# Attention in a gated cross-attention block: image copies on ScalarE, normalising on GpSimd, maxima of two PSUM banks at once

## What is computed

```python
ctx_img, ctx_txt = context[:, :257], context[:, 257:]
q = rms_norm(linear(x, q_w, q_b), norm_q_w)
k, k_img = rms_norm(linear(ctx_txt, ...)), rms_norm(linear(ctx_img, ...))
v, v_img = linear(ctx_txt, v_w, v_b), linear(ctx_img, v_img_w, v_img_b)
def attention(q, k, v):
    scores = jnp.einsum('bqhd,bkhd->bhqk', q, k) / sqrt(32)
    return jnp.einsum('bhqk,bkhd->bqhd', softmax(scores), v)
out = attention(q, k_img, v_img) + attention(q, k, v)
x = x + tanh(g_xattn[0]) * linear(out, o_w, o_b)
```

## Time and profile before

| | |
|---|---|
| Runs (3) | 1731.56 us median (1729.67 to 1732.33) |
| Profiled execution, first to last instruction | 1726.7 us |
| TensorE busy | 1689.0 us, 98%, granted clock at its upper level nearly throughout |
| VectorE | 1201.3 us, 70% |
| GpSimd | 901.7 us, 52% |
| ScalarE | 822.3 us, 48% |

### The profile page before, as it was taken

One profiled execution on the slowest core, in us unless ns is written; L12 is line 12 of the kernel. 1 busy time (PEld: TensorE's weight loads), 2 busy tenths in 40 slices (PEclk: granted clock), 3 DMA queues, 4 the chain that ended last, 5 costly groups with the idle time before them and its releaser, 6 DMA issues. The chain is left out here.

```text
span 1726.7 us, 24755 instructions
## 1 busy us (share of the span) xinstructions
PE 1689.0 (98%) x8694; PEld 1105.9 (64%) x8694; DVE 1201.3 (70%) x2250; ACT 822.3 (48%) x1520; POOL 901.7 (52%) x343
## 2 busy tenths in 40 slices
PE   6999999999999999999999999998999999999999
PEld 5888878885444445444544444445777778888777
DVE  6776677667888887888778888877555354443565
ACT  4433333236666664666556666662322355554221
POOL 3221312116777774787747777711515477675542
PEclk9999999999999999999999999999999999999999
DMA  9556858546555542554545445221313488876533
GB/s 330 165 165 196 229 182 211 180 164 192 138 151 146 145 134 57 147 151 132 148 122 127 111 131 142 84 93 42 134 37 134 159 266 271 261 264 211 166 109 98
DMA packets 198603, 273.04 MB, mean 158 GB/s; under 512 B 30968, under 2 KB 128008, under 8 KB 197964
## 3 DMA queue, kind: packets, MB, share of 16 engines
q1 hardware_dynamic: 192928, 254.61, 50.0%
q0 software_dynamic: 5120, 16.78, 2.9%
q10 hardware_dynamic: 432, 0.07, 0.0%
HBM read 198.15 MB, written 106.18 MB: 176 GB/s over the span
## 5 line engine op out<-in xcount | busy, mean ns | idle before, releaser
L1255 ACT ACTIVATE P<-ps 128x512 f32<-128x512 f32 (+1 forms) x832 | 444.4, 596 | 257.2 <-PE ps L1096 223.0
L640 DVE TENSOR_REDUCE mp<-ps 128x1 f32<-128x448 f32 x768 | 426.9, 613 | 83.9 <-PE ps L443 83.9
L1521 POOL TENSOR_TENSOR sacc<-sacc,P 128x2048 f32<-128x2048 f32 x90 | 396.3, 4403 | 17.5 <-ACT P L1255 6.9
L443 PE MATMUL ps<-Kst,Qst 96*128 96x448 f32 (+1 forms) x1024 | 382.6, 391 | 2.0 <-DVE mp L640 1.0
L443 PEld LDWEIGHTS ps<-Kst,Qst 96*128 96x128 f32 x1024 | 192.4, 188 | 210.8 <-DVE mp L640 150.5
L1096 PE MATMUL ps<-Qst,Kst 100*128 100x512 f32 (+1 forms) x832 | 321.2, 410 | 3.2 <-ACT P L1255 2.3
L1039 PE MATMUL ps<-P,Vg 128*32 128x512 f32 (+2 forms) x1664 | 216.2, 606 | 0.3 <-ACT P L1255 0.2
L822 POOL TENSOR_TENSOR cl<-craw,ch 128x1024 fp32r<-128x1024 f32 (+2 forms) x26 | 62.1, 2387 | 283.2 <-ACT ch L550 283.2
L1096 PEld LDWEIGHTS ps<-Qst,Kst 100*128 100x128 f32 (+1 forms) x832 | 151.8, 185 | 61.6 <-ACT P L1255 37.3
L49 PE MATMUL ps<-W,ch 128*128 128x512 f32 (+1 forms) x408 | 162.5, 398 | 0.0
L51 PE MATMUL ps<-W,cl 128*128 128x512 f32 (+1 forms) x408 | 159.7, 391 | 0.0
(11 more groups left out here) (245 smaller groups left out, 3072.0 us busy)
## 6 DMA issues: line engine op xcount, KB each, us to landing
gur<-in_w_gate_up SPq DMA_DIRECT2D x23, 1024.0 KB, 7.5
Kst<-KHd SPq DMA_DIRECT2D x56, 320.0 KB, 4.8
Vd<-vf SPq DMA_DIRECT2D x50, 256.0 KB, 2.1
craw<-in_ctxT SPq DMA_DIRECT2D x24, 512.0 KB, 4.5
KHd<-sth SPq DMA_DIRECT2D x24, 512.0 KB, 3.5
KLd<-stl SPq DMA_DIRECT2D x24, 512.0 KB, 4.8
dnr<-in_w_down SPq DMA_DIRECT2D x23, 512.0 KB, 3.9
xg<-Xg SPq DMA_DIRECT2D x23, 512.0 KB, 7.7
```

Source lines behind the costliest of these rows:

```text
L443: pe.matmul(ps[:, bank, 0:c1 - c0], Qst[G % 3][0:96, j, 128 * qt:128 * qt + 128], Kst[G % 2][0:96, j, c0:c1], start=True, stop=True).then_ ...
L640: dve.reduce_max(out, ps[:, bank, 0:c1 - c0], AX.X).then_inc(d_ra, 1)
L1255: act.activation(P[slot(G, kt)][:m, j, :], ps[:m, 2 + (e - 1) % 3, :], ACT.Exp, scale=SCALE).then_inc(a_exp, 1)
L1521: pool.tensor_tensor(sacc[:, h], sacc[:, h], P[slot(G, kt)][:, h], ALU.add).then_inc(g_sum, 1)
```

## The change

The image's weighed values and total are copied by ScalarE from PSUM (`img_weighed`, `img_total`), as the text's are. T and I now lie side by side in a new tile `ms` (its first eight rows also serve as `mrh` and `mrl`), go through DRAM and are inverted separately, so `rc` and both transfers double in size. GpSimd computes i/I, t/T and their sum, three instructions in place of two, and doesn't split; the low half is VectorE's, at tile 2. VectorE's three products are gone.

The 64 units become 35 events: 14 pairs of the first two text chunks of one block, 6 single ones, 7 pairs of the third chunk, 8 pairs of image chunks. A pair fills two neighbouring banks and is reduced by one instruction. The ring has two slots, banks (0, 1) and banks (6, 7). The weighing moves to bank 5, totals stay in bank 7, which is also the second bank of a slot; so the first twelve events are, in the slot of banks 6 and 7, single ones that use bank 6 alone.

```diff
-    BANKS_RA = (0, 1, 5)
-    UNITS = (7, 6, 3, 6, 5, 6, 6, 6, 6, 5, 6, 2, 0)
-    PLAN = [[1] * n + [0] * (7 - n) for n in UNITS]
+    PV, TOTALS = 5, 7
+    PLAN = [(1, 1, 1, 0, 1, 0, 0), (1, 1, 1, 1, 0, 0, 0), (1, 0, 0, 1, 0, 0, 0)]
+    PLAN += [(1, 1, 1, 0, 0, 0, 0)] * 8 + [(1, 0, 0, 0, 0, 0, 0), (0,) * 7]
+    def max_events():
+        b = [(j, qt) for j in range(4) for qt in range(4)]
+        wide = [((0, *x), (1, *x)) for x in b[:14]]
+        lone = [((c, *x),) for c in (0, 1, 2) for x in b[14:]]
+        third = [((2, *b[i]), (2, *b[i + 1])) for i in range(0, 14, 2)]
+        image = [((3, j, qt), (3, j + 1, qt)) for j in (0, 2) for qt in range(4)]
+        first = [x for w, o in zip(wide[:6], lone) for x in (w, o)]
+        return first + wide[6:] + third + image
+    def ring(n):
+        return (0, 1) if n % 2 else (6, 7)
...
-        def ra_bank():
-            if ra >= 68:
-                pe.wait_ge(d_ra, ra - 2)
-            return BANKS_RA[(ra - 65) % 3]
+        def ring_free(n):
...
+                pe.wait_ge(d_ra, n - 1)
...
+                if i == FIRST_IN_TOTALS and G >= 2:
+                    pe.wait_ge(a_img, 2 * (G - 1))
+                ring_free(ra)
+                for (c, j, qt), bank in zip(EVENTS[i], ring(ra)):
+                    c0, c1 = CH[c]
+                    ins = pe.matmul(ps[:, bank, 0:c1 - c0], Qst[G % 3][0:96, j, 128 * qt:128 * qt + 128],
+                                    Kst[s][0:96, j, c0:c1], start=True, stop=True)
+                ins.then_inc(p_ra, 1)
...
+        def img_weighed(G):
+            act.wait_ge(p_pv, pv_no(G, 12))
+            if G:
+                act.wait_ge(g_oi, 3 * G)
+            act.activation(oi[:], ps[:, PV, :], ACT.Copy).then_inc(a_img, 1)
+        def img_total(G):
+            act.wait_ge(p_tot, 5 * G + IMAGE_TOTAL)
+            act.activation(ms[:, 1, :], ps[:, TOTALS, :], ACT.Copy).then_inc(a_img, 1)
...
+            if kt == 2 and 0 < G < NG:
+                img_total(G - 1)
...
+                    if kt == 1 and j == 1 and G >= 1:
+                        img_weighed(G - 1)
+                        if G >= 2:
+                            split(G - 2)
...
-            elif kt == 1 and 1 <= G < NG:
...
-                dve.tensor_tensor(oi[:], ps[:, 6, :], rt2[:, pG % 2, :], ALU.mult).then_inc(d_oi, 1)
...
-            elif kt == 2 and 1 <= G < NG:
...
-                dve.tensor_tensor(rt2[:, pG % 2, :], rt2[:, pG % 2, :], ps[:, 7, :], ALU.mult).then_inc(d_img, 1)
+            elif kt == 2 and 2 <= G < NG:
+                units(G + 1, at, sum(plan))
+                split(G - 2)
...
+                dve.reduce_max(out, ps[:, bank:bank + k, 0:cols] if k > 1 else ps[:, bank, 0:cols], AX.X).then_inc(d_ra, 1)
...
+            dve.tensor_tensor(a_low(G), ot2[:, G % 2, :], a_high(G).bitcast(F32), ALU.subtract).then_inc(d_atl, 1)
...
-            pool.tensor_tensor(oi[:], oi[:], ot, ALU.add).then_inc(g_oi, 1)
-            pool.tensor_tensor(oi[:], oi[:], rt, ALU.mult).then_inc(g_oi, 1)
+            pool.tensor_tensor(oi[:], oi[:], rt2[:, 1, :], ALU.mult).then_inc(g_oi, 1)
+            pool.tensor_tensor(ot, ot, rt2[:, 0, :], ALU.mult).then_inc(g_oi, 1)
+            pool.wait_ge(g_oi, 3 * G + 2)
+            pool.tensor_tensor(ot, ot, oi[:], ALU.add).then_inc(g_oi, 1)
```

More of the change, by code:

```diff
@@ L80, in program @@
     mx = sb(p12, "mx", [128, 4, 2, 4], F32)
-    mrh = sb(p12, "mrh", [8, LQ], F32R)
-    mrl = sb(p12, "mrl", [8, LQ], F32R)
+    ms = sb(p12, "ms", [128, 2, LQ], F32)
+    mrh, mrl = ms[0:8, 0, :].bitcast(F32R), ms[0:8, 1, :].bitcast(F32R)
     s_const = sem("s_const")
@@ L217, in rows_ra @@
     def rows_ra(G):
-        return 64 + 65 * G + 4 * sum(x < G for x in (5, 9))
+        return 64 + 36 * G + 4 * sum(x < G for x in (5, 9))
     def head_rows(d, G, c0, c1):
@@ L1103, in weigh @@
                 if G:
[L1104 to L1107, removed]
+                    pe.wait_ge(a_img, 2 * G - 1)
             pe.wait_ge(a_exp, exp_no(G, kt, 3))
-            pe_heads(6, lambda j: Vg[s][p0:p1_, kt, 32 * j:32 * j + 32], P[slot(G, kt)], p0, p1_, first, last).then_inc(p_pv, 1)
+            pe_heads(PV, lambda j: Vg[s][p0:p1_, kt, 32 * j:32 * j + 32], P[slot(G, kt)], p0, p1_, first, last).then_inc(p_pv, 1)
         def total(G, kt, p0, p1_, first, last):
-            pe_heads(7 if G < NG - 1 else LAST_IMAGE, lambda j: ones[p0:p1_, :], P[slot(G, kt)], p0, p1_, first, last).then_inc(p_tot, 1)
+            pe_heads(TOTALS if G < NG - 1 else LAST_IMAGE, lambda j: ones[p0:p1_, :], P[slot(G, kt)], p0, p1_, first, last).then_inc(p_tot, 1)
         def text_end(G):
@@ L1135, in image @@
             pe.wait_ge(d_add, 4 * G + (4 if G < NG - 1 else 9))
-            pe_heads(7, lambda j: ones[:, :], sacc, 0, 128, False, True).then_inc(p_tot, 1)
+            pe_heads(TOTALS, lambda j: ones[:, :], sacc, 0, 128, False, True).then_inc(p_tot, 1)
         def image_total(G):
@@ L1185, in pe_attend @@
                     pe.wait_ge(d_ra, ra)
-                    pe_mrow(BANKS_RA[(ra - 65) % 3])
+                    pe_mrow(ring(ra)[0])
                     ra += 1
@@ L1288, in act_attend @@
                     if kt == 12 and j == 1 and G + 1 < NG:
-                        act_rows_high(G + 1, BANKS_RA[(rows_ra(G + 1) - 65) % 3])
+                        if G:
+                            act.wait_ge(s_den, 112 * (G - 1) + 16)
+                        act_rows_high(G + 1, ring(rows_ra(G + 1))[0])
             if step == NKT * NG - 1:
@@ L1359, in units @@
             for i in range(m, m + n):
-                dve_max_unit(i, ra, BANKS_RA[(ra - 65) % 3])
+                (c, j, qt), k = EVENTS[i][0], len(EVENTS[i])
+                bank, cols = ring(ra)[0], CH[c][1] - CH[c][0]
+                if c == 3:
+                    out = mx[:, qt, 1, j:j + k]
+                elif c == 2:
+                    out = mp[:, 4 * qt + j:4 * qt + j + 4 * k - 3:4, 2]
+                else:
+                    out = mp[:, 4 * qt + j, c:c + k]
+                dve.wait_ge(p_ra, ra + 1)
+                dve.reduce_max(out, ps[:, bank:bank + k, 0:cols] if k > 1 else ps[:, bank, 0:cols], AX.X).then_inc(d_ra, 1)
                 ra += 1
@@ L1435, in dve_attend @@
                 if more:
-                    dve_rows_low(G + 1, BANKS_RA[(ra - 65) % 3])
+                    dve_rows_low(G + 1, ring(ra)[0])
                     ra += 1
@@ L1441, in dve_attend @@
             if G in PROJECTED and kt in (4, 6, 8, 10):
[L1442 removed]
+                dve_project_tile(PROJECTED[G], (kt - 4) // 2, ra, ring(ra)[0])
                 ra += 1
@@ L1556, in pool_attend @@
                 normalise(G - 1)
-                if G == NG - 1:
-                    split(G - 1)
     sp_attend()
```

125 lines of the change are left out of this document (58 added, 67 removed).

## The result

| | before | after |
|---|---|---|
| Median of runs | 1730.62 us (1727.25 to 1732.33, 4 runs) | 1746.47 us (1744.18 to 1747.03, 4 runs) |
| Ratio to before | | 1.0087, 95% interval 1.0072 to 1.0101 |
| Profiled execution, span | 1726.7 us | 1745.0 us |
| VectorE busy | 1201.3 us | 1164.7 us |

The kernel is 0.9% slower. The time lies inside the range given (1716 to 1755) and on the likelier side, but 11 us above the 1735 forecast and outside the range of the forecast's own case (1729 to 1741).

A forecast was written before the change was run, and what follows sets the result against it. No engine is full; event order bounds the attention, GpSimd's sums filling nearly all of first sum to E. Group terms sum to +4 us: span 1726.7 to 1730.7, plus 4.9 outside, 1735.5, written as 1735; range 1716 to 1755.

The forecast's parts named there:

- the forecast's own case: Whole kernel: the summed terms hold, 1735 us, own range 1729 to 1741; chance 48%.
- Merged maxima and products: VectorE, each attention group: 29 fewer maxima instructions save 2.3 us, products less split 1.3; some 3.6 us less in all.
- the signs: Expected trace marks: VectorE busy 3 to 5 us a group lower, pairs about 1.07 us, plain period 46.9.
- Ring: Key tiles 3 to 8: two slots give 3.50 us a step, now 3.65; VectorE's saved time becomes idle time.
- E: Start of ScalarE's first exponential of key tile 11, ending the stretch from GpSimd's first sum; forecast 0.11 us later.
- The rival of the costlier ring: Two-slot ring costs more than 3.50 us a step, putting E 1 us later in 13 groups: 1748 us; chance 12%.
- Split: Tile 2: VectorE's low-half split arrives 0.45 us before the limit and delays GpSimd's next add 0.4 us; E +0.11.
- The rival of the late split: Split arrives after GpSimd's add began, VectorE stands still, E moves 3.3 us in 13 groups: 1778 us; chance 15%.
- Turnaround: From E to next first sum: mrl 1.1 us earlier, but tile 0's single waits for it; +0.02 against group 8.
- The other terms: Groups besides the plain ones: group 0 +1.2, group 1 +0.1, groups 5 and 9 +1.1 each, 14 -1.1, last +0.5.
- The last term: Time outside the span: 4.9 us, median 1731.56 less span 1726.7, added to span 1730.7 for 1735.5.
- the hidden wait: Rival: tile 0's single doesn't hold TensorE, 13 groups turn around 1.1 to 1.2 us faster: 1720 us; chance 20%.

The follow-up runs named there:

- the copies alone: Changed kernel's ScalarE copies, inverted totals, GpSimd steps and VectorE split, but 64 single maxima in three banks, old order; against the kernel before: 1733.40 us, ratio 1.0015.
- the control: Kernel before with every text weighing one step earlier, from tile 2 on: 1743.50 us, ratio 1.0064 to the kernel before.
- the wait alone: Kernel before with one wait added: at key tile 0 TensorE waits for mrl before weighing tiles 11 and 12; 1738.46 us, ratio 1.0042.

## Why the prediction came out as it did

*Merged maxima and products.* The pair's 1.085 us is right. VectorE's busy time in plain group 2 fell from 39.94 us to 38.02, by 1.9 and not by the 3.6 of the sum (3 to 5 among the signs); the 36.6 us of the whole kernel lie in part in other stages. The products' part was put at 1.3 (its terms add up to 1.2) and is 1.1 in the copies alone (38.82). The merges gave 0.8 where 2.3 was put: where the ring makes each pair wait, it runs for nearly its whole length, and the overlap with a neighbour that the 0.99 assumed is lost (three pairs take 3.20 us, 1.06 apart). That less of it came changed nothing. The Trainium skill's fixed part for a PSUM operand ("VectorE: DVE Perf Modes", fixed latency per instruction) gave an estimated 3.6 us a group; by durations the trace is near it (2 x 613 - 1085 = 141 ns a merge, 29 of them 4.1 us), by VectorE's busy time it isn't (0.8 us).

*Ring.* Forecast 3.50 us a step, measured 3.44 to 3.47 (starts of VectorE's rows of three, 806.12 and 809.56); E 32.5 us after the first sum, forecast 32.7. The rival of the costlier ring gave 1748, near the result, but by another mechanism: E didn't move. The number alone would have confirmed it.

*Split.* Forecast about 0.8 us and harmless, measured 922 to 984 ns in all twelve, GpSimd's run 27.41 instead of 27.09. The rival of the late split (+3.3 us) was right in kind; made real, it cost 4 to 6.

*Turnaround: the step that failed.* "VectorE is free before E, so mrl would end at E + 5.23 as in group 0: 1.1 us gained." It ended at E + 6.3. Two TensorE weight loads of the kernel before show why group 0 was no model, the weighing of tile 9 in group 0 and in group 8:

```profile
433.48 0.16 PEld L1039 LDWEIGHTS ps<-P,Vg 128*32 128x32 f32 x8 [0.24 <-issue]
...
822.44 0.16 PEld L1039 LDWEIGHTS ps<-P,Vg 128*32 128x32 f32 x8 [0.24 <-issue]
```

They start at E - 1.1 and at E + 0.6. VectorE's last image maxima, before in groups 0 and 8 and after in group 8:

```profile
432.24 1.42 DVE L640 TENSOR_REDUCE mx<-ps 128x1 f32<-128x258 f32 x4 [1.03 <-PE ps L443]
...
820.65 2.13 DVE L640 TENSOR_REDUCE mx<-ps 128x1 f32<-128x258 f32 x6 [0.89 <-PE ps L443]
```

```profile
830.38 0.70 DVE L1417 TENSOR_REDUCE mx<-ps 128x2 f32<-128x516 f32 x1 [0.26 <-PE ps L1107]
```

They end at E - 0.9, E + 0.9 and E + 0.3. In group 0 ScalarE had waited 1.56 us for GpSimd, and meanwhile TensorE and VectorE had both run ahead. After, VectorE was not quite free before E either; it was free 0.6 us earlier than before, and the low half moved by 0.1 only. TensorE's weighing starts at 831.23, E + 0.4, only 0.2 earlier than before. Leaving 1.0 us of TensorE's work out moved the low half by 0.65. So it is the lead of group 0, first of all TensorE's, that made the low half early there, and relief of VectorE couldn't bring it. The ring paragraph of the same prediction has it that "TensorE reaches E at about 821.9, as before", level with GpSimd, so the lead of group 0 was excluded there and used here. The loss side was sized nearly right (the single waits; 1.2 against group 0, and 1.0 measured by moving it), the gain side is 0 where 1.1 was put. Hence +1.06 a plain group instead of +0.13.

*The other terms.* Groups 5 and 9: +1.1 forecast, -0.1 measured. The wait costs 1.0 there too (59.7 without it), and a gain of as much, which the forecast denied them, pays for it; half of that comes with the copies alone (60.2). Where the rest comes from wasn't followed. Groups 14 and 15 up to the last exponential: -0.6 forecast, -1.3 measured, within what this stretch varies by. Group 0: +1.2 forecast, +2.9 measured. The single accounts for 1.76 (moved, 47.97 becomes 46.21). The rest, 1.1, isn't there with the copies alone (45.10); the section on the hardware has a candidate.

The sum: against the forecast, ten plain groups 9.3 us more, group 1 1.0, group 0 1.7, groups 5 and 9 2.4 less, the end 0.7 less: 9 more, the measured +13 against +4. The span is 14.3 above the forecast 1730.7, 9 by this and 5 by the experts. The last term, 4.9 us outside the span, was misread: it is the median of the runs less the span of one single execution. Where a run's own span is known it lies only 1.2 to 1.6 us below its time, so that execution was some 3.4 us faster than the median. That takes 3.4 back, and the median is 11 above 1735.5. That it still lies inside the range owes something to luck: the range was made wide for other mechanisms, the hidden wait and a costlier ring, and neither came about.

## What to carry to other kernels

An interval taken from a stage with slack may be used in another stage only after asking who was ahead there: read, for each engine, how far before or after the anchor it arrives. Where several chains reach a point level, the first forecast for shortening one alone is zero (GpSimd's here), and work moved from behind the point to ahead of it only changes sides. When a reused buffer is put at the head of an in-order queue, its wait is paid by everything behind it, and so is the work it guards; placing it one position later cost nothing here and gave 1 us a group back.

## What the runs showed of the hardware

*The clock.* Windows of the ends of the projections and the start of the attention, in the kernel before and after (columns as in the earlier trace rows, the granted clock third from the end):

```profile
392.00:396.00 4.00, 2.96 (x17) 2.04 (x15) 3.70 (x8) 2.50 (x4) 0.00 (x0) 1.00 0.32 119
396.00:406.00 10.00, 9.88 (x45) 4.66 (x43) 8.68 (x17) 7.42 (x14) 3.51 (x2) 1.00 0.66 212
```

```profile
392.00:396.00 4.00, 2.51 (x14) 1.57 (x13) 3.65 (x7) 1.17 (x2) 0.00 (x0) 1.00 0.48 172
396.00:406.00 10.00, 8.82 (x22) 6.18 (x21) 5.66 (x7) 6.50 (x11) 3.67 (x2) 0.51 0.60 198
```

After, TensorE ran at the lower level (1.2 of 2.4 GHz) for ten microseconds at the start of the attention, behind a stretch in which it had been busy 2.51 of 4 us instead of 2.96. It waited there 1.01 us for VectorE's low half of the last transposed keys (`stl`, L626, read from a bank that the second slot uses) and 0.48 us for the first maxima. The copies alone had the first of these waits too (1.03 us) and kept the upper level. Every kernel here with two slots shows a mean clock of 0.51 to 0.66 in that window, the kernel before, the copies alone and the control 1.00, and the wait alone 0.83. TensorE then came to the weighing of tile 9 of group 0 33.1 us after the first sum (435.44) instead of 31.0. About 4 us of the low stretch lie behind the first sum (402.33; the clock is 0.50 up to 406 and 0.90 in the next 2 us), an estimated 2 us of TensorE's time by the two levels. In the kernel with the wait alone the low stretch was over by 400, ahead of its first sum at 401.89, and group 0 grew by 0.6 like the others. So the clock fits the 1.1 us of group 0, but it isn't shown: no run took the drop away by itself, and every kernel in which it reaches past the first sum also has the two-slot ring, which may cost something of its own in group 0.

*The ports.* The split, a VectorE instruction with two SBUF operands, waits for the GpSimd add that is running: it took 0.93 us where it came 0.4 us before one ended (802.80 above), 4.23 where one had begun 0.9 us earlier (834.09 and 834.96 above), in all twelve cases of that kernel 4222 to 4315 ns. The two GpSimd adds around it took 9.51 us together instead of 9.1 (a third of 27.41), so it ran between them. The Trainium skill ("SBUF — State Buffer", "Who interferes with whom") has the rule: a VectorE instruction with two SBUF inputs contends with a GpSimd one that reads SBUF, and issue order decides who blocks. The trace agrees, and these runs give its price.
